# The ramp of a convolution and feed-forward kernel in another order: last taps behind all four convolutions, weights in three column parts

## The reference

```
K = 2.0 * einsum('hn,hnl->hl', Ct, exp(dtA[:, :, None] * arange(512))).real      # 32 x 512
y = irfft(rfft(u, 1024) * rfft(K, 1024))[..., :512] + u * D[:, None]
y = y * (arange(512)[None, :] < length[:, None])[:, None, :]
gate_out = fake_quant_fp8_linear(y, gate_w, ...)      # 512 -> 1376
up_out   = fake_quant_fp8_linear(y, up_w, ...)        # 512 -> 1376
hidden   = silu(gate_out) * up_out
out = x + fake_quant_fp8_linear(hidden, down_w, ...)  # 1376 -> 512
```

## Time and profile before

| | |
|---|---|
| median of 3 runs | 339.97 us (339.72 to 340.18) |
| the profiled execution's own time | 340.48 us |
| its span, first to last instruction | 338.8 us |
| PE busy | 309.3 us, 91% of the span |
| DVE busy | 304.8 us, 90% |
| ACT busy | 205.4 us, 61% |
| POOL busy | 11.3 us, 3% |
| mean granted TensorE clock | 0.995 of full speed |

### The profile page before, as it was taken

One profiled execution on the slowest core, in us unless ns is written; L12 is line 12 of the kernel. 1 busy time (PEld: TensorE's weight loads), 2 busy tenths in 40 slices (PEclk: granted clock), 3 DMA queues, 4 the chain that ended last, 5 costly groups with the idle time before them and its releaser, 6 DMA issues.

```text
span 338.8 us, 4808 instructions
## 1 busy us (share of the span) xinstructions
PE 309.3 (91%) x1564; PEld 159.8 (47%) x1564; DVE 304.8 (90%) x466; ACT 205.4 (61%) x312; POOL 11.3 (3%) x18
## 2 busy tenths in 40 slices
PE   0099799979999999999999999999999999899995
PEld 0056554434545554555445554555545454344442
DVE  5967979999999989998999899998999899997882
ACT  2527667729574757658583867476764968445530
POOL 2011000000000100010000100010001000000010
PEclk9999899999999999999999999999999999999999
DMA  7549997900000565016800672037600760070046
GB/s 234 100 128 226 258 311 161 349 9 1 2 0 0 101 197 201 2 15 136 343 0 0 124 284 87 0 58 195 242 2 1 136 238 0 0 126 0 2 67 182
DMA packets 12594, 38.27 MB, mean 113 GB/s; under 512 B 1344, under 2 KB 4000, under 8 KB 9632
## 3 DMA queue, kind: packets, MB, share of 16 engines
q1 hardware_dynamic: 8048, 26.48, 22.4%
q0 software_dynamic: 4528, 11.57, 19.2%
HBM read 33.80 MB, written 15.81 MB: 146 GB/s over the span
## 4 chain that ended last, share of the span: by engine, by line
PE 75%; DVE 12%; DMA 8%; issue 2%; ACT 1%; SPq 0%; POOL 0%; DVEq 0%
PE gate_ps L477 20%; PE up_ps L477 19%; PE down_ps L445 18%; PE y_ps L430 16%; DMA wu<-in_up 6%; DVE ht L788 2%; DVE hq L797 2%; DVE hv L780 1%; PE down_ps L520 1%; DMA toep<-kpad_scratch 1%; DVE yq L764 1%; DVE yt L753 1%; DVE hq L805 1%; DMA prm<-in_params 1%; DMA kpad_scratch<-hc 0%
## 5 line engine op out<-in xcount | busy, mean ns | idle before, releaser
L355 ACT ACTIVATE sil<-gate_ps,fac 128x512 f32<-128x512 f32 (+1 forms) x88 | 60.2, 686 | 88.9 <-PE gate_ps L477 86.0
L477 PE MATMUL gate_ps<-yq,wg 128*128 128x512 bf16 (+2 forms) x372 | 89.5, 363 | 5.2 <-DVE yq L771 2.9
L477 PE MATMUL up_ps<-yq,wu 128*128 128x512 bf16 (+2 forms) x372 | 89.5, 363 | 0.0
L430 PE MATMUL y_ps<-xt,toep 128*128 128x512 f32 (+3 forms) x256 | 82.1, 440 | 0.7 <-DMA wu<-in_up 0.7
L780 DVE SCALAR_TENSOR_TENSOR hv<-up_ps,fac,sil 128x512 f32<-128x512 f32 (+1 forms) x88 | 65.6, 745 | 16.4 <-ACT sil L355 12.1
L445 PE MATMUL down_ps<-wd,hq 128*128 128x512 bf16 (+1 forms) x308 | 79.2, 379 | 0.3 <-DVE hq L805 0.3
L477 PEld LDWEIGHTS gate_ps<-yq,wg 128*128 128x128 bf16 x372 | 35.9, 100 | 47.5 <-issue 5.1
L430 PEld LDWEIGHTS y_ps<-xt,toep 128*128 128x128 f32 x256 | 47.6, 193 | 22.5 <-issue 3.5
L477 PEld LDWEIGHTS up_ps<-yq,wu 128*128 128x128 bf16 x372 | 36.3, 100 | 38.3
L788 DVE SCALAR_TENSOR_TENSOR ht<-hc,hv 128x1024 f32<-128x1024 f32 (+1 forms) x48 | 54.1, 1127 | 0.2 <-ACT hc L338 0.2
L797 DVE SCALAR_TENSOR_TENSOR hq<-hc,ht 128x1024 bf16<-128x1024 f32 (+1 forms) x48 | 54.0, 1125 | 0.0
(11 more groups left out here) (134 smaller groups left out, 101.0 us busy)
## 6 DMA issues: line engine op xcount, KB each, us to landing
xt<-in_xT SPq DMA_DIRECT2D x8, 1024.0 KB, 7.7
toep<-kpad_scratch SPq DMA_DIRECT2D x7, 1024.0 KB, 9.7
out<-in_x SPq DMA_DIRECT2D x7, 1024.0 KB, 5.8
out<-res POOLq DMA_DIRECT2D x7, 1024.0 KB, 7.8
wd<-in_down POOLq DMA_DIRECT2D x1, 1280.0 KB, 23.0
wg<-in_gate POOLq DMA_DIRECT2D x1, 1120.0 KB, 12.3
wu<-in_up POOLq DMA_DIRECT2D x1, 1120.0 KB, 20.3
toep<-kpad_scratch SPq DMA_DIRECT2D x4, 256.0 KB, 3.7
```

The costliest lines, as they stand in the source:

```text
L355: nc.scalar.activation(sil[b][0:w, :], gate_ps[b][0:w, :], ACT.Silu, scale=fac[0:w, S_GATE:S_GATE + 1]).then_inc(silu_done, 1)
L430: last = nc.tensor.matmul(y_ps[h % 2][:, d * P:L], toep[par][:, h, d * P:(d + 1) * P], xt[par][:, h, 0:L - d * P], start=(d == 0), stop=(d ...
L477: mm = nc.tensor.matmul(ps[b][0:w, cols], wt[:, k, c * P:c * P + w], yq[par][:, version, k, cols], start=(k == 0), stop=(k == LB - 1))
```

## The change

The last filter group `k_of(2)` stands behind all four convolutions of block 0 and goes into the down banks instead of the up banks; its copy on ACT stands behind the roundings' inputs of all four channels instead of the first. `krow` lies elsewhere in memory, so that it lives longer. Block 1's second convolution stands whole behind `by_channel(1)`, where before three of its four steps stood behind `by_channel(2)` and the fourth in slot 0. On DVE the roundings of block 0 are written out in an order of their own: each mask stands between a rounding and its clip, the mask of block 1's channel 1 stands ahead of slot 0, and the sum, rounding and clip of its channel 0 stand inside slots 0 and 1. The later weights come in two parts instead of one (384 and 736 columns); PE waits for the first of them where it waited for all, and for the second in slot 5. SP loads the next x once block 0 is convolved and waits for the stored filter behind that load, not ahead of it; the other engines' waits for the stored filter move or go.

```diff
--- before.py
+++ after.py
@@ -47,7 +47,7 @@
 ROW = 640
 K_GROUPS = [slice(0, FIRST), slice(FIRST, 6), slice(6, JC)]
 WARM = 8
-EARLY = 2 * P
+EARLY, MIDDLE = 2 * P, 5 * P
 READ = 1
 EMPTY = 2
 UP20 = 2.0 ** 20
@@ -141,13 +141,13 @@
         dec = inside(hq[0], 0, JC, M)
         gu, gv = inside(hq[1], 0, JC, 2, KA), inside(hq[1], 2 * JC * KA, JC, 2, KA)
         gk = inside(hq[1], 4 * JC * KA, JC, 2, KA)
-        krow = inside(hc[0], 0, C, KB)[0:KA]
+        krow = inside(hq[1], 6 * JC * KA, C, KB)[0:KA]
         parts = [slice(0, FIRST), slice(FIRST, JC)]
         halves = [slice(0, N), slice(N, P)]
 
         params_in, scales_in = sem("params_in"), sem("scales_in")
         gate_in, up_in = sem("gate_in"), sem("up_in")
-        weights_in, down_in = sem("weights_in"), sem("down_in")
+        middle_in, weights_in, down_in = sem("middle_in"), sem("weights_in"), sem("down_in")
         xt_in = [sem(f"xt_in{i}") for i in range(2)]
         conv_in = [sem(f"conv_in{i}") for i in range(2)]
         copied = [sem(f"copied{i}") for i in range(2)]
@@ -181,8 +181,8 @@
         def k_in_bank(i, half):
 
             js = K_GROUPS[i]
-            bank = (down_ps, gate_ps, up_ps)[i][half]
-            return bank[0:KA, 0:(js.stop - js.start) * KB].rearrange("p (j b) -> p j b", b=KB)
+            bank, lo = (down_ps, gate_ps, down_ps)[i][half], (0, 0, 2 * KB)[i]
+            return bank[0:KA, lo:lo + (js.stop - js.start) * KB].rearrange("p (j b) -> p j b", b=KB)
 
         def rows_of_k(i, half):
             return krow[:].rearrange("p (j f) b -> p j f b", f=2)[:, K_GROUPS[i], half]
@@ -232,8 +232,10 @@
                 load_x_t(g, par)
                 load_toep(g, par)
 
+            sp.wait_ge(y_ready, HB)
+            load_x_t(2, 0)
             sp.wait_ge(k_stored[2], 16)
-            next_conv(2, 0)
+            load_toep(2, 0)
             copy_x(0, 0)
             next_conv(3, 1)
             copy_x(1, 1)
@@ -261,8 +263,10 @@
             pool.dma_start(wg[:, :, 0:EARLY], wg_d[:, :, 0:EARLY]).then_inc(gate_in, 16)
             pool.dma_start(wu[:, :, 0:EARLY], wu_d[:, :, 0:EARLY]).then_inc(up_in, 16)
             pool.wait_ge(toep_first[HB - 1], 16)
-            pool.dma_start(wg[:, :, EARLY:], wg_d[:, :, EARLY:]).then_inc(weights_in, 16)
-            pool.dma_start(wu[:, :, EARLY:], wu_d[:, :, EARLY:]).then_inc(weights_in, 16)
+            pool.dma_start(wg[:, :, EARLY:MIDDLE], wg_d[:, :, EARLY:MIDDLE]).then_inc(middle_in, 16)
+            pool.dma_start(wu[:, :, EARLY:MIDDLE], wu_d[:, :, EARLY:MIDDLE]).then_inc(middle_in, 16)
+            pool.dma_start(wg[:, :, MIDDLE:], wg_d[:, :, MIDDLE:]).then_inc(weights_in, 16)
+            pool.dma_start(wu[:, :, MIDDLE:], wu_d[:, :, MIDDLE:]).then_inc(weights_in, 16)
             pool.wait_ge(conv_in[1], 16)
             pool.dma_start(wd[:, 0:CH - 1, :],
                            wd_d[0:(CH - 1) * P, :].rearrange("(k p) n -> p k n", p=P)).then_inc(down_in, 16)
@@ -372,12 +376,9 @@
                 else:
                     act.wait_ge(ym_done, 1)
                 magnitude_y(0, h)
-                if h == 0:
-                    copy_k(2)
+            copy_k(2)
             scale_y(1, 0)
             magnitude_y(1, 0)
-            for stored_k in k_stored:
-                act.wait_ge(stored_k, 16)
             slots(0, 0, None, True, 2)
             with act.Fori(0, (NBLK - 4) // 2) as j:
                 slots(2 * j + 1, 1, j, False, 2)
@@ -465,6 +466,8 @@
                     b = (par + c) % 2
                     w = width(c)
                     if not (isinstance(n, int) and n < 2):
+                        if c * P == MIDDLE and not down:
+                            pe.wait_ge(weights_in, 32)
                         at_least(pe, silu_done, n - 1)
                         at_least(pe, prod_done, n - 1)
 
@@ -479,25 +482,25 @@
                                 if hi == HB:
                                     mm.then_inc(ready, 1)
                     for step, h, distances in CONV_PLAN.get(c, ()):
-                        if step <= ahead:
+                        if step <= ahead and (down or (step, h) != (1, 1)):
                             conv(g + step, (par + step) % 2, half + (1 if step == 2 else par), h, distances)
                     if down:
                         down_part(g - 1, 1 - par, c)
 
-            conv(0, 0, 0, 0, [0, 1, 3, 2])
+            for h in range(HB):
+                conv(0, 0, 0, h, [0, 1, 3, 2])
             k_of(2)
-            for h in range(1, HB):
-                conv(0, 0, 0, h, [0, 1, 3, 2])
-            pe.wait_ge(k_copied, 2 * len(K_GROUPS))
+            pe.wait_ge(k_copied, 4)
             pe.wait_ge(up_in, 16)
             by_channel(0)
             conv(1, 1, 0, 0, [0, 1, 3, 2])
             by_channel(1)
+            conv(1, 1, 0, 1, [0, 1, 3, 2])
             by_channel(2)
-            conv(1, 1, 0, 1, [0, 1, 3])
             by_channel(3)
-            pe.wait_ge(weights_in, 32)
+            pe.wait_ge(middle_in, 32)
             slots(0, 0, 0, False, 2)
+            pe.wait_ge(k_copied, 2 * len(K_GROUPS))
             pe.wait_ge(down_in, 32)
             with pe.Fori(0, (NBLK - 4) // 2) as j:
                 slots(2 * j + 1, 1, j, True, 2)
@@ -824,7 +827,12 @@
                         rounded(m - 2, g - 1, 1 - par, PAIRS - 2)
                     if c == 1 and not first:
                         rounded(m - 1, g - 1, 1 - par, PAIRS - 1)
-                    if c in MASK_PLAN and MASK_PLAN[c][0] <= ahead:
+                    if first and c == 0:
+                        sum_y(1, 0)
+                    elif first and c == 1:
+                        round_y(1, 1, 0)
+                        clip_y(1, 1, 0)
+                    elif c in MASK_PLAN and MASK_PLAN[c][0] <= ahead:
                         mask_y(g + MASK_PLAN[c][0], MASK_PLAN[c][1])
                     if c == 1 and not first:
                         clip(m - 2, 1 - par, PAIRS - 2)
@@ -845,19 +853,26 @@
             v.tensor_scalar(yv[0][:, 0, :], ym[0][:], f(D_GATE), None, ALU.mult)
             link(v.tensor_scalar(yv[0][:, 1, :], ym[0][:], f(D_UP), None, ALU.mult))
             mask_y(0, 1)
-            for h in range(HB):
-                sum_y(0, h)
-                if h + 2 < HB:
-                    mask_y(0, h + 2)
-                round_y(0, 0, h)
-                if h + 2 == HB:
-                    mask_y(1, 0)
-                clip_y(0, 0, h)
-            sum_y(1, 0)
-            round_y(1, 1, 0)
-            clip_y(1, 1, 0)
+            sum_y(0, 0)
+            round_y(0, 0, 0)
+            mask_y(0, 2)
+            clip_y(0, 0, 0)
+            sum_y(0, 1)
+            round_y(0, 0, 1)
+            mask_y(0, 3)
+            clip_y(0, 0, 1)
+            sum_y(0, 2)
+            round_y(0, 0, 2)
+            clip_y(0, 0, 2)
+            sum_y(0, 3)
+            mask_y(1, 0)
+            round_y(0, 0, 3)
+            clip_y(0, 0, 3)
+            mask_y(1, 1)
             dve.wait_ge(k_ready, 2 * len(K_GROUPS))
             slots(0, 0, True, 2)
+            for stored_k in k_stored:
+                dve.wait_ge(stored_k, 16)
             with dve.Fori(0, (NBLK - 4) // 2) as j:
                 slots(2 * j + 1, 1, False, 2)
                 slots(2 * j + 2, 0, False, 2)
```

## The result

The changed kernel takes 336.28 us (median of 6 runs, 335.87 to 336.68). The kernel before took 340.9 us in the 6 runs taken with it, three of them at 339.72 to 340.18 and three at 341.63 to 341.68; the ratio is 0.9871, 95% interval 0.9852 to 0.9890. In the later comparisons, with more runs, its median was 340.25 to 340.47. The forecast was 336.2 us, range 335.4 to 338.0, with 3.7 us gained; measured are 4.0 to 4.2 us against these later medians, and 4.4 where both kernels were run side by side once more.

The account below looks back on a forecast made before the run. DVE's chain to channel 3's clip was taken to bound the ramp, PE the blocks behind it. Slot 4's product moving from 55.18 to 51.45 gives 3.7 us: 339.97 - 3.7 = 336.2 us, range 335.4 to 338.0.

Parts of the forecast that it names:

- What bounds the ramp: Before block 1, DVE's chain to channel 3's clip bounds; from block 1 PE does, 37.20 us a block.
- The walk along DVE: Block 0 into the slots: DVE operations priced one by one; product of slot 4 at 51.45 instead of 55.18.
- The filter group's place: First convolutions: 1.42 us of filter matmuls leave PE's path, second mask starts at 26.9 instead of 28.34.
- The weights in three parts: Slots: first part lands at about 33, second at 45; the wait at 45.49 goes; late-weights rival 0.04.
- the second as before at 45: Later weights, needed in slot 5 at 53.2: by bytes they land at 45, as before the change.
- pieces down to 1 KB cost no rate: Weight transfers: 8.3 and 8.5 KB a microsecond an engine for both piece sizes, so landings are reckoned by bytes.
- The cited rule: Trainium skill on DMA queues: engines go round queues by packets, so small packets get less; spoke for the late landings.
- the sum: Slot 4's product: 55.18 - 51.45 = 3.7 us gained, kept whole to the end; chance as summed 0.68.
- SP's queue: Block 2's toep behind the filter's store: issued by 46, there by 60.1, costs nothing; late-toep rival 0.06.
- The clock: PE around 40 us: longest wait one microsecond, clock stays full; rival of a fall costs 0.7 to 2.5 us, chance 0.08.

Follow-up runs that it names:

- second profile: Both kernels run and profiled once more, nothing altered: changed kernel 335.98 us, kernel before 340.34 us.
- two kernels with three parts and the x early: Kernel before with only the weights in three column parts, 340.15 us; changed kernel with the last filter group again between first and second convolution, 338.21 us.
- three parts alone: Kernel before with only the weights in three column parts: 340.15 us, ratio 0.9977 to the kernel before.
- filter group last: Kernel before with only the last filter group moved behind all four convolutions, with its banks, copy, load order and waits: 337.78 us, ratio 0.9917.
- second warm-up of the kernel before: Kernel before with eight more warm-up matmuls ahead of the filter's first group, so that it warms up twice: 340.23 us, ratio 1.0002.
- DVE's order of before: Changed kernel with sum, rounding and clip of block 1's channel 0 ahead of the first product, mask of channel 1 in slot 0: 337.91 us.

## Why the prediction was right, and where it was off

**What bounds the ramp.** Right: DVE's chain to the last clip, then PE unbroken. From the product of slot 4 on, 20.01 us against the forecast's 20.02; the block of the steady part is 37.20 us before and after.

**The walk along DVE.** Forecast and trace: mask of channel 1 at 26.9, measured 27.31 and in the second profile 26.68; first product 42.05, measured 42.51 and 41.88; product of slot 4 at 51.45, measured 51.88 and 51.25; block 1 at 71.6, measured 72.03 and 71.41. The two profiles lie on both sides of each, together with their first mask (25.15 and 24.52). DVE's idle time ahead of the first product was forecast as 1.0 us and is 1.08. Undone one by one, the parts cost 1.9 us (filter group), 1.6 (DVE's order), 1.05 (weights) and about 0.6 (convolution), more than the 4.2 us together: they overlap.

**The filter group's place.** Right in the whole change: the second mask follows the first by 2.16 us instead of 3.77. But its weight was not seen. Alone it gave 2.7 us where I expected nothing, because I took the weights' landing as given.

**The weights in three parts.** Right that no wait takes the place of the one at 45.49. The first part landed at 35.3 (24.97 + 10.3, forecast 33), the rest at 42.95. Two steps did not hold. One is "the second as before at 45": with the store moved to 37.56, the x behind it does not run beside the weights. The other is "pieces down to 1 KB cost no rate". It holds where the weights are alone: in 2 us 0.43 MB went through in pieces of 2240 bytes (before, 36 to 38 us), 0.42 in pieces of 1472 (changed, 36 to 38) and 0.40 in pieces of 768 (changed, 32 to 34). Beside the x it does not: in the two kernels with three parts and the x early, the last part landed at 47.8 and 50.3 instead of 45.4, and the second is at the high end of the prediction's range for it, 41 to 50.4. The cited rule was thus the better guide, and that the changed kernel has its weights at 42.95 is luck as far as the prediction goes. Neither step moved the sum, since slot 5 needs the last part only at 53.

**SP's queue.** Right: store at 37.56 (forecast 37.1), 6.3 us to land (at most 8.8), toep issued at 43.84 (by 46) and at most 10.6 us under way. PE never waits for it.

**The clock.** Right: 1.00 from 36 to 50 us. For the kernel before, 61 runs have a mean clock on record. 14 show 0.998 or more and have a median of 340.26 us, 29 show 0.994 or 0.995 and have a median of 340.31: a single fall costs its median nothing that can be told. The 18 runs at 0.993 or less have 11 of the 12 times above 341 us, up to 343.38. The ten runs of the changed kernel are all at 0.998 or more. So the long times of the kernel before go with lower clocks; that the clock is their cause is shown by one profile, the second, and argued for the rest.

**The size.** Forecast 3.7, measured 4.0 to 4.4. Block 1 starts 3.3 and 3.9 us earlier in the two profiles than in the first profile of the kernel before, and from the first mask it is 3.9 in both, 0.2 more than the sum. Another 0.5 us lies between the start of block 1 and the end of the span: 263.46 us in both profiles of before and 263.4 with the three parts alone, 262.95 to 263.0 in the changed kernel and in all those with its place for the filter in memory, its order of loads on SP and its moved waits. PE's last steps are equally far from the start of block 1 in all of them; the difference lies behind the last residual on DVE, 2.9 us to the end before and 2.4 after. No term of the prediction has it, and its cause stays open; without it the changed kernel would have gained about what was forecast.

## What to carry to other kernels

When two things bound a stretch one right behind the other, try each on its own from both sides: added alone, the filter group's place gave 2.7 us and the three weight parts 0.3; undone alone, the parts cost 0.6 to 1.9. A transfer's landing is not a constant: a store of many small pieces at the head of another queue brought a 1.1 MB load in 2.7 us earlier, because it held back a load with large pieces. Beside such a load, smaller pieces land later. On the engine that bounds, order by what the others wait for first, and expect nothing from filling an idle gap with work that delays that.

## What the runs showed of the hardware

**Two queues share by packets.** In stretches of 2 us in which both queues had work, they moved nearly the same number of packets, whatever their size: 64 and 63 (2.2 KB of weights, 8 KB of x, the kernel before, 40 to 42 us), 283 and 284 (weights and the store, filter group last, 40 to 42), 71 and 78 (1.5 KB of weights, x, three parts alone, 38 to 40).

**The pace early in the kernel.** In the profile of the changed kernel the warm-up matmuls ahead of the first convolution follow each other by 0.43 us, twice the 0.22 us of the same matmuls in the second warm-up of the kernel before: the pace of the 1.2 GHz level, while the granted clock of 16 to 24 us is given as 1.00. In the other traces the pace rises in the last of the warm-up matmuls or in the first convolution, at a time that varies: the first mask comes at 24.03 to 25.15 us over the traces. In the changed kernel this goes straight into the end: 25.15 and 24.52 in its two profiles, with spans of 335.0 and 334.4 us.

**Falls of the clock.** In six traces the granted clock fell to 0.50, the 1.2 GHz level, at the end of or behind a wait of PE of 1.90 to 2.53 us in the stretch from 37 to 46 us. It did not follow each such wait: behind the 2.26 us wait of the kernel before it fell in one profile and not in the other, where it fell only with the 2.53 us wait for the weights. With waits of up to 1.83 us there (DVE's order of before) it did not fall in any.
